# Gathered attention with its logits laid out by key, and a routed mixture with rows kept per expert and blocks scattered to the output

## What is computed

```python
def gathered(q, kv, Wq, Wkv, Wc):          # q: 4 x 512 x 128, kv: 4 x 77 x 128
    qp = q @ Wq.T
    idx = argmax(qp @ kv.T, axis=-1)       # every token picks one of 77 context rows
    mk, mv = split(kv[idx] @ Wkv.T, 2)     # keys and values of 8 features, shared by the heads
    logits = qh @ mk.T / sqrt(8)           # 16 heads of 8 features
    return concat(softmax(logits) @ mv) @ Wc.T

def mixture(x, centroids, ln_g, ln_b, w1, b1, w2, b2):    # 2048 tokens, 8 experts
    aff = x @ centroids.T
    eid = argmax(aff);  alpha = sigmoid(max(aff))
    xln = normalise(x) * ln_g[eid] + ln_b[eid]
    return x + alpha * (relu(xln @ w1[eid] + b1[eid]) @ w2[eid] + b2[eid])
x = x + gathered(layernorm(x), ctx, ...)
x = x + mixture(layernorm(x), ...)
```

## Time and profile before

| | us |
|---|---|
| median of 3 runs (2223.18 to 2225.08) | 2223.51 |
| the profiled execution | 2226.05 |
| its span in the trace | 2224.2 |
| first two stages | 0 to 1820 |
| gathered attention | 1820 to 2046 |
| mixture | 2046 to 2224 |

### The profile page before, as it was taken

The page is one execution under the profiler, slowest core; times in us unless marked ns, Lnnn a source line. Parts: engine busy times, 40 slices in busy tenths (PEclk is TensorE's granted clock), DMA queues, the critical chain, the costliest instruction groups (busy, mean ns, idle before and its releaser), DMA issues. The chain is left out here.

```text
span 2224.2 us, 76642 instructions
## 1 busy us (share of the span) xinstructions
PE 1968.2 (88%) x31783; PEld 1328.2 (60%) x31783; DVE 1461.0 (66%) x2646; ACT 1401.0 (63%) x2766; POOL 1411.5 (63%) x1800
## 2 busy tenths in 40 slices
PE   5659999999999999999999999999999967887293
PEld 4526666666666666666666666666666645554262
DVE  2367777777778778787776877777877635333421
ACT  1167787677776777777777777777777722332041
POOL 1167888778887788887788877888778610001302
PEclk9779999999999999999999999999999966555596
DMA  2011111112110021101201112111101100001311
GB/s 90 0 25 38 61 45 29 38 29 75 32 38 29 29 82 32 31 28 38 76 29 31 29 38 76 28 31 32 34 29 29 31 7 0 1 0 32 99 40 47
DMA packets 55114, 82.88 MB, mean 37 GB/s; under 512 B 13140, under 2 KB 40042, under 8 KB 54002
## 3 DMA queue, kind: packets, MB, share of 16 engines
q1 hardware_dynamic: 53746, 75.88, 11.5%
q0 software_dynamic: 1024, 2.10, 0.3%
HBM read 25.66 MB, written 5.11 MB: 14 GB/s over the span
## 5 line engine op out<-in xcount | busy, mean ns | idle before, releaser
L1068 PE MATMUL b_bank_proj<-layer_weights,b_stream_t 128*128 128x512 f32 x1152 | 588.5, 612 | 34.2 <-DVE b_plain_moved L942 18.1
L942 DVE TENSOR_TENSOR b_plain_moved<-b_bank_proj,b_rope 128x1024 f32<-128x1024 f32 x384 | 463.9, 1219 | 189.0 <-ACT b_squares L828 137.1
L753 POOL TENSOR_TENSOR b_rotated<-b_plain_moved 128x1024 f32<-128x1024 f32 x192 | 453.8, 2363 | 23.6 <-DVE b_plain_moved L942 18.6
L768 POOL TENSOR_TENSOR b_rotated<-b_rotated,b_inv_norm 128x1024 f32<-128x1024 f32 x192 | 365.3, 1903 | 15.6
L859 ACT ACTIVATE b_k_t<-b_bank_shared 64x512 f32<-64x512 f32 x384 | 226.5, 590 | 125.9 <-PE b_bank_shared L1076 123.5
L828 ACT ACTIVATE b_squares<-b_bank_proj 128x512 f32<-128x512 f32 x384 | 229.3, 597 | 115.6 <-PE b_bank_proj L1068 111.2
L1068 PEld LDWEIGHTS b_bank_proj<-layer_weights,b_stream_t 128*128 128x128 f32 x1152 | 186.1, 191 | 135.9 <-issue 44.9
L773 POOL TENSOR_TENSOR b_probs<-b_probs,b_inv_sum 128x512 f32<-128x512 f32 x192 | 200.5, 1045 | 87.2 <-DVE b_inv_sum L963 85.8
L1076 PE MATMUL b_bank_shared<-const_tables,b_rotated 128*128 128x128 f32 x1536 | 233.2, 277 | 22.0 <-POOL b_rotated L768 21.9
L850 ACT ACTIVATE b_q_t<-b_bank_shared 64x512 f32<-64x512 f32 x384 | 225.6, 588 | 34.3 <-PE b_bank_shared L1076 31.5
L1076 PEld LDWEIGHTS b_bank_shared<-const_tables,b_rotated 128*128 128x128 f32 x1536 | 178.1, 141 | 113.4 <-issue 99.2
(11 more groups left out here) (319 smaller groups left out, 2929.1 us busy)
## 6 DMA issues: line engine op xcount, KB each, us to landing
b_v_shifted<-b_v SPq DMA_DIRECT2D x96, 384.0 KB, 3.5
layer_weights<-L_ffn_Wqkv SPq DMA_DIRECT2D x6, 1536.0 KB
b_v_shifted<-b_v SPq DMA_DIRECT2D x72, 128.0 KB, 3.4
d_w<-L_ffn_w SPq DMA_DIRECT2D x16, 256.0 KB, 5.6
layer_weights<-L_ffn_Wo SPq DMA_DIRECT2D x6, 512.0 KB
layer_weights<-L_ffn_W SPq DMA_DIRECT2D x6, 341.0 KB
sorted_rows<-d_zero SPq DMA_DIRECT2D x1, 1472.0 KB, 7.6
expert_rows<-d_sorted_out SPq DMA_DIRECT2D x23, 64.0 KB, 1.5
```

The source lines that it names most:

```text
L753: nc.gpsimd.tensor_tensor(out=turned[:, k, :], in0=pm[:, k, 0, :], in1=pm[:, k, 1, :], op=ALU.add).then_inc(add_done, 1)
L768: nc.gpsimd.tensor_tensor(out=tk, in0=tk, in1=repeat_last(rn[:, k, :], DH), op=ALU.mult).then_inc(rope_done, 1)
L942: nc.vector.tensor_tensor(to, src.to_broadcast(shape), tab.to_broadcast(shape), ALU.mult).then_inc(mul_done, 1)
L1068: nc.tensor.matmul(out, xs[:, b, t * P:(t + 1) * P], w, start=True, stop=True).then_inc(proj_full, 1)
```

## The change

Gathered attention:
- The logits are computed twice, in two layouts. Once by token, as before but from two halves of 64 rows, only for their maximum (`highest`, DVE, negated); the maxima are transposed on PE and copied by ACT into spare rows of two query tiles, `low` and `high`. Then again by key, directly as 77 keys x 128 tokens per head: 16 matmuls whose stationary side `kbd` has a row of ones for the head's negative maximum. ACT takes the exponent straight from that bank into `probs_t`.
- The subtraction on DVE, the separate exponent and the 16 transposes are gone.
- Only element 0 passes the front before the loop. The fronts of the elements 1 to 3 are cut in pieces (`normed`, `queries`, `scores`, `counts`) that share bank `bk_l[3]` and stand in the rounds of the element before. `kbd` is built by POOL (two products of 128x616 per element).
- SP fills a larger HBM buffer (17280 rows of 258 numbers) from a constant row whose last number is a token number outside the output; its nine DMAs are issued behind the stage's loads, and SP waits for them at the end of the stage.

Mixture:
- Every expert owns 16 blocks of rows in the buffer, so a token's row is known from its rank alone, per batch element; `places(b)` and the scatter of element `b` don't wait for the totals. A row holds 128 normalised numbers, 128 of the sum to be kept, the gate, and the token's number (258 numbers, 1032 bytes). POOL makes the sums.
- SP reads a block's place from SBUF and loads blocks one by one (23 DMAs).
- `hidden` has the expert's `w1` stationary (copied by ACT out of the dynamic place) and yields the transposed result at once; the four transposes are gone. DVE forms `alpha * result + sum` per block.
- POOL scatters each block straight to the output, with rows of empty places dropped by a bounds check. The store to `expert_rows`, the gather and the last addition are gone.
- A second clearing of semaphores stands at the start of the gathered stage.

```diff
                 def probs_t(u, q):
-                    pe.wait_ge(exp_done, 2 * u + q // 2 + 1)
+                    b, t = u // TILES, u % TILES
+                    if q == 0:
+                        pe.wait_ge(max_done, u + 1)
                     wait(pe, pT_done, 4 * u + q - 1)
                     for n in range(GROUP):
-                        last = nc.tensor.transpose(bk_t[q % 2][0:CTX, n * P:(n + 1) * P], pr[:, u % 2, GROUP * q + n, :], ident)
+                        a, h = q // 2, (q % 2) * GROUP + n
+                        last = nc.tensor.matmul(bk_t[q % 2][0:CTX, n * P:(n + 1) * P], kbd[:, b, a, h, :],
+                                                stacks[a][:, b, t * P:(t + 1) * P], start=True, stop=True)
...
+                empty = const_h[:, C_EMPTY:C_EMPTY + ROW]
+                for i in range(0, REGION, NT):
+                    n = min(NT, REGION - i)
+                    to = sorted_h[i * P:(i + n) * P, :].rearrange("(i p) d -> p i d", p=P)
+                    sp.dma_start(to, repeat_mid(empty, n)).then_inc(emptied, 16)
+                sp.wait_ge(emptied, 16 * -(-REGION // NT))
...
-                pool.wait_ge(y_out, 16 * BLOCKS)
-                for u in range(NT):
-                    pool.indirect_dma_start(yg[:, u, :], None, expert_h[:, :],
-                                            bass.IndirectOffsetOnAxis(ap=pos[:, u:u + 1], axis=0)).then_inc(y_in[u // TILES], 16)
+                def store(i):
+                    pool.wait_ge(to_done, i + 1)
+                    pool.wait_ge(y_done, i + 1)
+                    pool.indirect_dma_start(out_rows, bass.IndirectOffsetOnAxis(ap=to[:, i:i + 1], axis=0),
+                                            y[:, i, :], None, bounds_check=NT * P - 1, oob_is_err=False).then_inc(stored, 16)
...
+                for i in range(BLOCKS):
+                    at = sp.value_load(place[0:1, i:i + 1], min_val=0, max_val=REGION - 1)
+                    sp.dma_start(xin[:, i:i + 1, :], sorted_rows[:, bass.ds(at, 1), :]).then_inc(x_in[i], 16)
...
-                def hidden(i, e):
+                def hidden(i):
                     pe.wait_ge(xT_done, i + 1)
-                    wait(pe, h_done, i - 1)
-                    nc.tensor.matmul(bk_h[i % 2][:, :], xT[:, i % 2, :], w1s[:, bass.ds(e, 1), :].rearrange("p o n -> p (o n)"),
-                                     start=True, stop=True).then_inc(h_full, 1)
...
+                        last = nc.tensor.matmul(bk_h[i % 2][f // 2][:, (f % 2) * P:(f % 2 + 1) * P],
+                                                own[:, i % 2, f * P:(f + 1) * P], xT[:, i % 2, :], start=True, stop=True)
+                    last.then_inc(h_full, 1)
```

More of the change, by code:

```diff
@@ L1289, in gathered_attention @@
         scale = float(np.float32(1.0) / np.sqrt(XDH).astype(np.float32))
+        half = P // 2
+        sides = (slice(0, half), slice(half, P))
+        maxes = (slice(half, half + SIDE), slice(0, SIDE))
+        stacks = (low, high)
+        pieces = [("normed", 0), ("queries", 0), ("scores", 0), ("normed", 1), ("counts", 0)]
+        before = []
+        for u in range(NT):
+            before.append(len(pieces))
+            b, t = u // TILES, u % TILES
+            if t == 0 and b + 1 < B:
+                pieces += [("queries", b + 1), ("scores", b + 1)]
+            if t == 1 and b + 1 < B:
+                pieces.append(("counts", b + 1))
+            if t == 3 and b + 2 < B:
+                pieces.append(("normed", b + 2))
+        nth = {p: n + 1 for n, p in enumerate(pieces)}
         def by_tile(a, b):
@@ L1605, in _ @@
                     if u < NT:
-                        probs_t(u, 0)
                         probs_t(u, 1)
                     if 1 <= u <= NT:
-                        by_token(u - 1)
-                    if u + 1 < NT:
-                        logits(u + 1)
+                        attended(u - 1)
+                    if t == 0 and b + 1 < B:
+                        queries(b + 1)
                     if u < NT:
@@ new lines, in _ @@
+                first(0)
+                pool.wait_ge(up_in, 16)
+                nc.gpsimd.tensor_copy(rows[:, :, 2 * P + 1], tokens).then_inc(token_done, 1)
+                for b in range(B):
+                    if b + 1 < B:
+                        first(b + 1)
+                    second(b)
+                    summed(b)
+                pool.wait_ge(token_done, 1)
+                for b in range(B):
+                    scatter(b)
+                token(0)
+                for i in range(BLOCKS):
+                    if i + 1 < BLOCKS:
+                        token(i + 1)
+                    store(i)
@@ new lines, in rectified @@
+                def rectified(i):
+                    act.wait_ge(h_full, i + 1)
+                    wait(act, y_full, i - 2)
+                    if i == 0:
+                        act.wait_ge(col_done, 1)
+                    for f in range(2):
+                        last = nc.scalar.activation(hT[:, i % 3, f * P:(f + 1) * P], bk_h[i % 2][0][:, f * P:(f + 1) * P], ACT.Relu,
+                                                    bias=colv[:, 2 + f, i:i + 1])
+                    last.then_inc(ra_done, 1)
@@ L1801, in result @@
[L1801 to L1811 removed]
+                for i in range(BLOCKS):
+                    rectified(i)
+                    if i + 2 < BLOCKS:
+                        weights(i + 2)
```

733 lines of the change are left out of this document (400 added, 333 removed).

## The result

The changed kernel takes **2116.6 us** (median of 4 runs, 2110.97 to 2118.46); the kernel before took 2223.35 beside it. The ratio is 0.9515, with a 95% interval of 0.9496 to 0.9534. The forecast was 2134 (2110 to 2168). The profiled execution is one of 2118.46 us; its span happens to be 2116.6 too, against 2224.2: 107.6 us less, where the sum was 89.9 less. So the direction and the range held, and 17.7 us more came than were summed. What follows says from which terms.

The account below looks back on a forecast made before the run. The prediction took the gathered loop as bound by a ring of hand-overs at half clock, the block loop by PE. Terms -49.9 (gathered), -2.5, -6.5 and -31 (mixture) sum to -89.9, from 2223.51 to 2134 us, range 2110 to 2168.

Parts of the forecast that it names:

- The gathered round: Gathered loop: PE's work at full clock sums to 7.5 us, taken as 7.8 a round instead of 11.7, for 16 rounds.
- rival E: Whole kernel: less than summed, with passes of 0.11 us and a front 3 us shorter; 2119 us or less; 10%.
- the hand-over that I added: Gathered loop: 0.3 us a round added to PE's summed work for hand-overs, giving 7.8.
- Pieces, front and way out: Gathered stage: fronts of elements 1 to 3 cost 14 us, loop starts at 1851.7, way out 6, slow start 3.
- Clearing stores: Gathered stage: 17415 KB of stores take 90 us, or 180 read the other way, ending between 1913 and 2003.
- Rival A: New gathered loop: clock stays at 1.2 GHz, a round takes 14 us, 2245 us in all; 4%.
- B: Gathered loop: hand-overs among DVE, ACT and PE still count, round 9.5 instead of 7.8, +27 us, 2161; 15%.
- C: Gathered logits: 64-row passes lose what four groups of 32 rows gave, eight take 2.05 us, +10, 2144; 10%.
- D: POOL's bounded stores in the block loop (+16 us) or the clearing stores (+7) bind; both 2157; 8%.
- Head, scatter and load: Mixture before its block loop: scatter starts 3.4 us earlier, its waits cost +1, load unchanged; sum -2.5 us.
- Block loop: Mixture's loop of 23 blocks: 2.8 us a block, 68.6 us instead of 75.1, -6.5.
- Tail: Mixture's end after the last block: 4.5 us instead of 35.5, -31.

Follow-up runs that it names:

- the first experiment: Two kernels with half the change each: new gathered stage without clearing stores before the old mixture, 2162.1 us; old gathered stage with those stores before the new mixture, 2184.2 us.
- e3: Changed kernel with the 16 matmuls of logits by key in each round replaced by 16 transposes; span 2110.7 us, round 5.86 us.
- e8: e6 with the 16 two-pass matmuls of logits by key in each round replaced by 32 one-pass transposes; 2235.1 us.
- e6: New gathered stage without clearing stores, old mixture, plus two pauses on PE in each of 15 rounds; 2243.9 us.
- e11: Kernel before, with each of the 16 transposes of the probabilities in a gathered round issued twice; 2210.2 us.
- e12: Kernel before, with each of the 16 transposes of the probabilities in a gathered round issued as a two-pass matmul with the identity; 2209.1 us.
- e10_short_waits: New gathered stage without clearing stores, old mixture, PE's order changed so that it stands four times a round for a hand-over; 2252.5 us.

## Why the prediction came out as it did

*The gathered round, 7.8 summed, 6.92 measured.* This is the term that was mis-sized: 16 x 0.88 = 14.1 us, all of the 13.4 that the stage gave beyond the sum. Two things went into it. The first, 0.6 us, is what the groups of passes cost. In sum the 32 passes took 3.69 instead of 4.0, logits and `attended` together 2.24 instead of 2.57, `out` 0.23 instead of 0.28, and `attended_tt` 0.21 instead of 0.11: 6.91 instead of 7.5. A part of that is how I read a duration. The duration of a group runs to the end of its last pass, and the next group starts before that end: `attended` has 1.06 in the round above, but 1.00 from start to start; the logits 1.31 and 1.24; a group of eight passes of 128 columns 1.10 or 1.04, and 0.87 to 0.96. The Trainium skill's page "TensorE: Matmul & The Clock Gate", section "Back-to-back issue gap", says that a stream of matmuls is to be costed by the gap from start to start, not by the latency of one; the trace agrees, with 1.00 against 1.06.

But for logits and `attended` that is only 0.13 of the 0.33; the rest is that the rows I took were dearer themselves, 1.41 and 1.16 against 1.31 and 1.06. For `attended` show no full clock throughout: from 1865.50 to 1866.10, within that row, the granted clock is 0.80. The 1.11 behind my upper bound of 0.139 had no overlap in it, as the steps of a chain adjoin (2181.25 + 1.11 = 2182.36); there it was the choice of 0.125, in the middle of the bounds, that cost 0.3. The passes took 0.109 to 0.120, near the lower bound, as rival E had it. The second thing, the other 0.3, is the hand-over that I added and that isn't there.

*Pieces, front and way out.* Right. The three rounds with pieces are 9.45, 8.72 and 7.59 us long, 5.0 more than three plain ones in all; that times three is 15, where 14 was summed. The loop began at 1849.73, 31.7 after the stage's begin, where 1851.7, 31.5 after the begin of before, was forecast. Way out and the slow start of the loop are what is left, 8.3 for 9.

*Clearing stores.* Right: hidden, as both halves of the first experiment show.

*Rival A.* Its chance was small, and it didn't come. But the reason given for that was half wrong. That transposes don't count was taken as borne out by 0.50 at a PE that is 91% busy; e3, e8 against e6, and e11 against e12 speak against it. The rule of the Trainium skill's page "TensorE: Matmul & The Clock Gate", Part 4, that was weighed there, is not what these kernels do. The other half, that the new loop has no wait of a microsecond, came true, but no run shows it to be the reason: the old ring's own waits were 0.70 and 0.31, and e10_short_waits stood at 0.86 with one of 1.27 in each round. So 1.00 was right, and in part by luck: half of its reason was wrong and the other half is not shown.

*Rivals B, C, D.* The ring was gone: PE never stands for DVE or ACT in a plain round. C is treated above, and so is the half of D on the clearing. Of its other half, POOL is busy 23.58 of 50 us in the block loop while PE is busy 50.00, so its stores don't bind. *Rival E*, given 10%, came nearest in its total, 2119 against 2116.6, and in its pass, but not in how it got there: with 8 us less over 16 rounds its round was 7.3, still 0.4 too long, and its front, 3 us shorter, did not come. That its number fits is in part luck.

*Head, scatter and load, -2.5 summed, +0.1 measured.* The first scatter starts 31.8 us after the mixture's first DVE row (before 33.65): -1.9 instead of -3.4. One part of that is probably DVE, which stands still beside POOL's sums (last section); how much of it lay on the way to the scatter no run shows. The scatter is 28.6 us from first to last issue instead of 27.0, since its five waits are 2.0 to 2.4 instead of 1.8: +1.6 for +1. The load path has the register load in it, +0.4.

*Block loop, 68.6 summed, 63.7 measured.* Again the price of eight passes was too high. A block takes 2.505 us: `hidden` 1.00 from start to start (2061.15 to 2062.15), the transpose 0.11, `result` 0.98, the bias 0.42. I had 1.11, 0.11, 1.11 and 0.41 and then rounded up to 2.8: 22 x 0.3 = 6.5 too much; the slow first blocks took 1.6 more than I gave them. Of the 0.13 by which `result` was too dear, 0.05 is the reading, for in the timeline of the kernel before the same group starts 1.06 us ahead of the next:

```profile
2178.15 1.13 PE L2028 MATMUL d_bank_bank<-d_w,d_hidden_t 128*128 x8
2179.21 0.48 PE L2030 MATMUL d_bank_bank<-d_b,d_block_onehot_wide 8*128 8x128 f32 x2
```

The other 0.08 is that the same eight passes follow each other faster in the new loop, for which no run gives a reason.

*Tail.* Right to a tenth, 4.5.

## What to carry to other kernels

Cost a stream of matmuls by the distance between the starts of its groups, in rows that stand at one clock from end to end: for the groups of eight passes here the durations were 5 to 20% above the distances. That was a part of the error only; too dear a price for a pass, over 16 rounds and 23 blocks, came to most of it. The old ring of hand-overs was paid for twice, once in waiting and once in the clock, so that taking it out was worth more than its waits, and even adding idle passes to it was a gain. Not every ring does that (e10_short_waits, with more waiting, stood at 0.86), so read the granted clock of the loop before pricing it. And if software-issued DMAs show a wait at a fixed count of issues, as here at every fourth, room for descriptors is a cause to test: with twice the room it came at every eighth.

## What the hardware showed that was not expected

The clock first: 16 useless passes a round made the old loop faster (216.4 instead of 227.3 us), and whether they were transposes or matmuls made no difference.

The second is how hard POOL's work can hit DVE. Beside two memsets of 128x2048 (1.80 us each, from 1826.06 to 1829.60) and a smaller one behind them four small DVE steps that took 1.12 us for the element before took 4.36; beside `summed`, four additions of 8 elements took 1.85, where those of the last element, without POOL beside them, took 0.77. Those rows in the changed kernel's timeline of DVE, without the one of 1.12 us:

```profile
1826.14 4.36 DVE L1479 TENSOR_SCALAR c_normed<-residual,c_mean_var,c_rstd 128x128 f32<-128x128 f32 x4 [1.48 <-POOL c_rstd L1343]
...
1995.82 1.85 DVE L2011 TENSOR_TENSOR d_tokens_before<-d_tokens_before,d_onehot 128x8 f32<-128x8 f32 x4
...
2017.89 0.77 DVE L2011 TENSOR_TENSOR d_tokens_before<-d_tokens_before,d_onehot 128x8 f32<-128x8 f32 x4
```

The Trainium skill's page "SBUF — State Buffer" describes the pair of ports that the two share as a lock held for a whole instruction; the trace agrees: of DVE's four steps, which began beside the memsets, one alone takes 3.79 us, where the median of such a step is 0.34, and it ends just after the last memset does at 1829.86.
